# A transformer block on one core: text rows loaded in two parts, patch rows computed directly, and the last 36 keys' three products stacked into one

## The reference

```python
x = jnp.einsum('bnd,ed->bne', x, proj_w) + proj_b + pos_embed     # patches
h = jnp.concatenate([h, txt], axis=1)                             # (8, 164, 192)
xn = layernorm(layernorm(h), ln_w)
Q = xn[:, None] * W_qk[None, :, None, :]                          # 12 heads
attn = softmax(where(causal, Q @ Q.T / sqrt(192), -inf))
out = attn @ (xn - mean(wte, axis=0))                             # wte: 50257 x 192
out = out / arange(1, 165); out = concat_heads(out) @ W_o.T
h = h + out
```

## Time and profile before

| | us |
|---|---|
| median of 3 runs | 373.03 (372.75 to 373.41) |
| the profiled execution | 372.14, its span 370.40 |
| TensorE busy | 332.7 (90% of the span) |
| DVE / ACT / GpSimd busy | 219.9 / 127.9 / 169.0 |
| mean granted TensorE clock | 0.976 |
| bytes moved | 74.29 MB, mean 201 GB/s |

### The profile page before, as it was taken

The page is one execution under the profiler, slowest core; times in us unless marked ns, Lnnn a source line. Parts: engine busy times, 40 slices in busy tenths (PEclk is TensorE's granted clock), DMA queues, the critical chain, the costliest instruction groups (busy, mean ns, idle before and its releaser), DMA issues.

```text
span 370.4 us, 6796 instructions
## 1 busy us (share of the span) xinstructions
PE 332.7 (90%) x2352; PEld 306.4 (83%) x2352; DVE 219.9 (59%) x546; ACT 127.9 (35%) x438; POOL 169.0 (46%) x181
## 2 busy tenths in 40 slices
PE   5886779999799899899899898999949999999992
PEld 1866679989699799799798798999824999999991
DVE  1479638678669679578588888656476222222221
ACT  2065423644643453454436004545720111111110
POOL 3067375583574763862953501450562134444321
PEclk9899889999999999999999999999998999999997
DMA  7399999899799899799797999900223599999930
GB/s 226 114 419 341 215 213 212 236 177 210 221 196 213 225 199 239 191 199 271 162 198 155 295 229 237 230 11 0 84 101 93 165 276 276 273 265 272 273 93 15
DMA packets 20176, 74.29 MB, mean 201 GB/s; under 512 B 3388, under 2 KB 9021, under 8 KB 18874
## 3 DMA queue, kind: packets, MB, share of 16 engines
q0 software_dynamic: 7344, 30.57, 40.8%
q1 hardware_dynamic: 9898, 40.40, 36.8%
q10 hardware_dynamic: 2912, 3.04, 2.9%
HBM read 66.12 MB, written 9.25 MB: 203 GB/s over the span
## 4 chain that ended last, share of the span: by engine, by line
PE 39%; issue 18%; DMA 14%; POOL 14%; DVE 8%; ACT 3%; POOLq 1%; SPq 0%; DVEq 0%; ACTq 0%
PE bO L1198 18%; DMA wbuf<-in_wte 11%; PE bE L1198 10%; PE bS L1198 5%; PE bJ L1198 4%; POOL AwA L390 4%; DMA H<-in_txtA 4%; POOL PA L416 3%; POOL wbuf L401 3%; POOL AwB L390 2%; ACT PA L552 2%; POOL PB L416 1%; DVE negmax L791 1%; PE bT L1544 1%; DVE PTB0L L808 1%
## 5 line engine op out<-in xcount | busy, mean ns | idle before, releaser
L552 ACT ACTIVATE PA<-bS,negmax 128x128 f32<-128x128 f32 x96 | 33.9, 366 | 85.2 <-DVE negmax L791 85.2
L416 POOL TENSOR_TENSOR PA<-PA,rn 128x512 f32<-128x512 f32 x24 | 25.8, 1075 | 64.3 <-DVE rn L803 64.3
L390 POOL TENSOR_TENSOR AwA<-zT,w 96x512 f32<-96x512 f32 x45 | 53.4, 1514 | 3.3 <-ACT zT L534 3.3
L1198 PE MATMUL bJ<-wo_sb,oTA 128*128 128x192 f32 x288 | 51.4, 328 | 0.0
L1198 PEld LDWEIGHTS bS<-zT,AwA 96*128 96x128 f32 x384 | 48.0, 197 | 1.1
L1198 PE MATMUL bS<-zT,AwA 96*128 96x128 f32 x384 | 48.2, 280 | 0.0
L1198 PEld LDWEIGHTS bJ<-wo_sb,oTA 128*128 128x128 f32 x288 | 46.2, 190 | 0.0
L1198 PE MATMUL bO<-PA,wx 96*128 96x112 f32 x384 | 45.4, 275 | 0.5 <-DVE PA L1171 0.5
L1198 PEld LDWEIGHTS bO<-PA,wx 96*128 96x128 f32 x384 | 44.9, 192 | 0.7 <-DVE PA L1171 0.7
L463 POOL DMA_INDIRECT out<-PA,yrow x16 | 15.0, 940 | 56.1 <-DVE PA L1187 56.1
L689 ACT ACTIVATE AwA<-bO 128x448 f32<-128x448 f32 x16 | 8.7, 543 | 78.4 <-PE bO L1198 52.8
(11 more groups left out here) (247 smaller groups left out, 690.9 us busy)
## 6 DMA issues: line engine op xcount, KB each, us to landing
wbuf<-in_wte POOLq DMA_DIRECT2D x20, 1344.0 KB, 13.0
wx<-in_wi SPq DMA_DIRECT2D x16, 576.0 KB
wx<-in_wo SPq DMA_DIRECT2D x16, 576.0 KB
wx<-in_wte SPq DMA_DIRECT2D x6, 1344.0 KB, 8.5
dispatched<-zeros SPq DMA_DIRECT2D x7, 675.5 KB, 10.3
wbuf<-in_wte SPq DMA_DIRECT2D x2, 1344.0 KB, 12.1
AwA<-dispatched ACTq DMA_DIRECT2D x14, 168.9 KB
wo_sb<-in_wo_attn SPq DMA_DIRECT2D x1, 1728.0 KB, 6.9
```

What stands on the lines that cost most here:

```text
L390: nc.gpsimd.tensor_tensor(o, zT[:, k, ss].unsqueeze(1).to_broadcast(list(o.shape)), w2[:, k, hs].unsqueeze(2).to_broadcast(list(o.shape)), ...
L416: nc.gpsimd.tensor_tensor(t, t, q.unsqueeze(2).to_broadcast(list(t.shape)), ALU.mult).then_inc(p_ready, 1)
L552: last = nc.scalar.activation(PA[:, h, :], bank[:, j * SA:(j + 1) * SA], ACT.Exp, bias=negmax[:, h:h + 1], accum_out=lsum[:, h:h + 1])
L1198: return nc.tensor.matmul(o, l, r, start=start, stop=stop, skip_group_check=True)
```

## The change

1. The text rows are loaded as 80 and 12 partitions in place of 92. The patches and their weights are loaded in two halves.
2. TensorE computes the patch rows of batches 0 and 1 directly, without embT. The other batches' transposes stand between score(0, 1) and score(0, 2). Twelve warming products (`stay_warm`) before and behind the first z_transpose are gone. pat_sb, pw_sb and embT lie in expert buffers.
3. The first two table chunks go ahead of wo_attn; SP waits for all of ACT's first constants before them. The matrices for the routing are loaded after the plain chunks, and ACT casts them in batch LAST-1.
4. On GpSimd the weighing stands in front of the table loads. Statistics and factors of batches 2 to 7 move from the start into batch 0.
5. B rows are held three times on 108 partitions (txtB is loaded three times). PB has 108 further columns per group, into which `last_keys` writes the last 36 keys' normalised probabilities three times; p_transpose(b, 4) transposes them at once. In PTB1 and vB the partitions hold high and low parts so that one product with 128 partitions is the sum of all three.

```diff
+SR = 3 * SB
+LV, LP = slice(0, SB), slice(64, 64 + SB)
 def pt_round(q, x, bank):
-            return PTB1[x][0:SB, :, :], bank[0:SB, 0:HEADS * SB]...
+            rows = LP if x else slice(0, SR)
+            return PTB1[rows, :, :], bank[rows, 0:HEADS * SB]...
 # SP
-            sp.dma_start(pw_sb, projw).then_inc(pat_in, 16)
-            sp.dma_start(pat_sb, patches).then_inc(pat_in, 16)
-            sp.dma_start(H[IMG:128, 0:NBATCH, :], txtA).then_inc(txt_in, 16)
+            for part, arrived in ((slice(0, 3), pat_in), (slice(3, 6), pat2_in)):
+                sp.dma_start(pw_sb[:, part, :], projw[:, part, :]).then_inc(arrived, 16)
+                sp.dma_start(pat_sb[:, part, :], patches[:, part, :]).then_inc(arrived, 16)
+            for p0, p1 in ((IMG, 116), (116, 128)):
+                sp.dma_start(H[p0:p1, 0:NBATCH, :], txtA[p0 - IMG:p1 - IMG]).then_inc(txt_in, 16)
+            sp.dma_start(H[0:BP, NBATCH:SLOTS, :], txtBp).then_inc(late_in, 16)
-            sp.wait_ge(hb_in, 16)
+            sp.wait_ge(hb_in, 48)
+            sp.wait_ge(w_in, 32)
-            sp.dma_start(wo_sb[:, :, :], wo_attn).then_inc(wo_in, 16)
             for s in range(WBUF):
                 sp.dma_start(wchunk[s], wv[:, s, :]).then_inc(wte_first, 16)
+            sp.dma_start(wo_sb[:, :, :], wo_attn).then_inc(wo_in, 16)
...
+            plain_loads(sp)
             sp.dma_start(mat32, cst2_d[:, C_MAT:NCST2]).then_inc(mat_in, 16)
-            plain_loads(sp)
 # GpSimd
-                        t, q = PB[:, q0:q0 + 2, :], rn[0:HB * SB, 12 + q0:14 + q0]
+                        t, q = PB[:, q0:q0 + 2, 0:SA], rn[0:HB * SB, 12 + q0:14 + q0]
+            def last_keys():
+                for q0 in (0, 2):
+                    t, k = PB[:, q0:q0 + 2, SEQ:SEQ + SR].rearrange("p q (t s) -> p q t s", t=3), PB[:, q0:q0 + 2, SA:SEQ]
+                    nc.gpsimd.tensor_tensor(t, k.unsqueeze(2).to_broadcast(list(t.shape)),
+                                            rn[0:HB * SB, 12 + q0:14 + q0].unsqueeze(2).unsqueeze(3).to_broadcast(list(t.shape)),
+                                            ALU.mult).then_inc(pb_ready, 1)
-            weigh(0, 1, (1,), range(3))
-            rsqrt(rstd[:, :, 2:NBATCH], nmr[:, :, 2:NBATCH], 2)
-            weigh(0, 1, (1,), (3,))
-            normalise(0, range(1))
+            weigh(0, 1, (1,))
             add_wte(2, 0, 0)
-            normalise(0, range(1, 2))
             add_wte(3, 1, 0)
-            normalise(0, range(2, 3))
+            normalise(0, range(3))
             def iteration(b, i, r):
                 normalise(b, range(3, SPR))
+                weigh(b + 1, n, (0, 1), (0, 1))
+                if r is not None:
+                    add_wte_nth(i, r)
+                last_keys()
+                weigh(b + 1, n, (0, 1), (2,))
+                normalise(b + 1, (0,))
+                if is0(b):
+                    rsqrt(rstd[:, :, 2:NBATCH], nmr[:, :, 2:NBATCH], 2)
+                if r is not None:
+                    add_wte_nth(i, r + 1)
+                normalise(b + 1, (1,))
+                weigh(b + 1, n, (0, 1), (3,))
+                if r is not None:
+                    add_wte_nth(i, r + 2)
+                normalise(b + 1, (2,))
 # ACT
-            act.dma_start(hB[:], txtB).then_inc(hb_in, 16)
+            for t in range(3):
+                act.dma_start(hB[t * SB:(t + 1) * SB, :, :], txtB).then_inc(hb_in, 16)
-                for v, z, n in ((vA, zA, 128), (vB, zB, SB)):
+                for v, z, n in ((vA[0], zA, 128), (vB, zB, SR)):
 # DVE: the first batch
             add_patches(0)
-            dve.wait_ge(txt_in, 16)
+            add_patches(1)
+            dve.wait_ge(txt_in, 32)
             z(0)
-            for j in range(1, 4):
-                add_patches(j)
-            variances(2, NBATCH)
-            row_max(0, 0)
...
+            row_max(0, 0)
             row_max(0, 1)
             row_factor(0, 0)
-            value_low(0)
+            for j in range(2, 5):
+                add_patches(j)
             row_factor(0, 1)
             row_max(0, 2)
+            value_low(0)
             z(1)
             row_factor(0, 2)
-            factors(2, NBATCH, 2)
 # DVE: iteration(b)
                 e_copy(b, 2)
+                if is0(b):
+                    variances(2, NBATCH)
                 plain_sum(b, 0)
                 row_max(b + 1, 0)
...
+                if is0(b):
+                    factors(2, NBATCH, 2)
                 z(b + 2)
 # TensorE
+            def embed_rows(b, k0, k1):
+                for k in range(k0, k1):
+                    last = mm(bT[b][0:IMG, 0:EMB], pat_sb[:, k, b * IMG:(b + 1) * IMG], pw_sb[:, k, :], k == 0, k == 5)
-                            last = nc.tensor.transpose(bank[0:SB, g * HS:(g + 1) * HS], PB[:, g, SA:SEQ], ident[0:HS, 0:HS])
+                            last = nc.tensor.transpose(bank[0:SR, g * HS:(g + 1) * HS], PB[:, g, SEQ:SEQ + SR], ident[0:HS, 0:HS])
-                        mm(oo, vA[x][:, 0:E0], PTB0[y][:, :, :], i == 0, False)
-                        last = mm(oo, vB[x][:, 0:E0], PTB1[y][:, :, :], False, i == 2)
+                        last = mm(oo, vA[x][:, 0:E0], PTB0[y][:, :, :], i == 0, False)
+                if g == 3:
+                    last = mm(oo, vB[:, 0:E0], PTB1[:, :, :], False, True)
-            stay_warm(bS[0], 6)
             z_transpose(0, 0)
-            stay_warm(bS[0], 6)
+            embed(bO[1][0:EC, EF:NBATCH * IMG], 1, EF, NBATCH * IMG).then_inc(emb_ready, 1)
             pe.wait_ge(bf_ready, 3)
-            for r in range(3):
-                score(0, r, r < 2)
+            score(0, 0, True)
+            score(0, 1, True)
+            pe.wait_ge(embT_ready, 2)
+            for j in range(1, 4):
+                token_transpose(j)
+            score(0, 2)
```

## The result

The changed kernel takes 375.96 us (median of 8 runs, 372.65 to 380.05) against 373.22 (372.08 to 373.87), a ratio of 1.0064 with a 95% interval of 1.0040 to 1.0088. The forecast was 356.3 us, with a range of 351 to 364.

A forecast was written before the change was run, and what follows sets the result against it. TensorE's own instructions were taken to bound the loop, plus one GpSimd wait, after a start waiting for data. Savings 4.8 + 2.0 + 2.3 + 6.2 + 1.4 = 16.7 from 372.14 gave 355.4, plus 0.89 for the median: 356.3 us, range 351 to 364.

The forecast's parts named there:

- Settled batches, 4 x 1.56: Four settled batches: each 1.56 us shorter (0.84 + 0.92 - 0.2), so -6.2 us in all.
- the 12 us pair: GpSimd's table loads reusing a slot after 12 us: only these could land late, by some 2 us; charged 0.
- Removal of the AwA wait and the 0.84 us of products: TensorE per batch: the 0.92 us wait for AwA goes, and value(b,3) saves 0.84 us of products.
- The start, -4.8: Up to the first PB normalisation: 35.4 us in place of 40.23, -4.8 us (bounds -0.5 and -6.5).
- Rival B: The start gains little: txtB's copies land at 12.5 us, zA at 20.0; 360.5 us in all; chance 0.10.
- Batch 0, 27.6: First interval of PB normalisations: 27.6 us in place of 29.63, without the chunk stall but with variances added; -2.0 us.
- Batch 1, 24.6: Second interval: 24.6 us in place of 26.89, the mat cast moving to where ACT waits anyway; -2.3 us.
- Behind the loop, -1.4: After the settled batches: two more shortened value(b,3), worth 0.84 and 0.6, so -1.4 us.
- A: The loop: the accumulating stream becomes the bound, 25.6 us a batch, five intervals lose 1.0; 361 us; chance 0.12.
- C: value(b,3): products saved do not shorten the loop, since it waits on other steps; seven times 0.84, 362 us; chance 0.07.
- D: TensorE's clock near z_transpose(0): idle time lowers it, two scores cost 2.8 us more; 359.1 us; chance 0.08.
- E: Slower: a batch's first load finds its slot not landed, TensorE stops at p_transpose(b,4), 4.8 us each; chance 0.07.

The follow-up runs named there:

- e2: The changed kernel with a second buffer for the plain table chunks; 363.78 us, ratio 0.975.
- e1: The changed kernel with GpSimd's three table loads back in front of the weighing and normalisations, one plain buffer; 370.76 us, ratio 0.997.
- e9: The kernel before with two buffers for the plain chunks and nothing else; 374.37 us, ratio 1.005.
- e10: The changed kernel, one plain buffer, with row_max(b+1,0) in front of plain_sum(b,0) on DVE; 367.48 us, ratio 0.984.
- e3: The kernel before with part 5 of the change alone (the stacked last keys); 373.19 us, ratio 1.002.
- e7: e2 with part 5 undone: one copy of txtB, three products again, no last_keys; 365.71 us, ratio 0.982.
- e12: e5 with last_keys in front of GpSimd's first table load of a batch; 357.77 us, ratio 0.958.
- e4: e2 with txtB's three loads behind the constants and statistics of only two batches before the patches; 364.27 us, ratio 0.977.
- e6: e4 with last_keys in front of GpSimd's first table load of a batch; 367.19 us, ratio 0.983.
- e14: e12 with only the variances' last instruction, nmr, moved behind row_max(1,1); 359.89 us, ratio 0.962.
- e8: e5 with the variances of batches 2 to 7 moved behind row_max(1,1); 361.65 us, ratio 0.970.
- e13: e12 with the variances of batches 2 to 7 moved behind row_max(1,1); 359.91 us, ratio 0.966.
- a0: The changed kernel, unedited, measured and profiled again; 380.13 us, ratio 1.014.
- e5: e2 with the three copies of txtB laid out in the input and loaded by one transfer; 362.81 us, ratio 0.973.

## Why the prediction was wrong

- **Settled batches, 4 x 1.56: failed, and the largest error** (7.2 us, with 3.3 in batch 1). The step is "What is late next? ... Only the 12 us pair can be late ... I take 0". It looked at GpSimd's own slots and not at the other load of the table. The sum was at hand: before, 16.5 us from the first plain_sum of a batch to the next issue (101.30 to 117.78) and 8.4 of landing are 24.9 of 26.2. Of the 16.5, the changed kernel needs 14.7, which with 8.4 would be 23.1; at the forecast's 24.6 only 1.5 are left, and the loads were moved towards the plain one, which then took 11.5. Shown by e2, e1, e9 and e10. The cycle accounts for the settled batches at full clock (26.06 on average); the rest of the 26.41 is the clock behind the wait that the cycle makes.
- **Removal of the AwA wait and the 0.84 us of products: right.** No wait for AwA in the changed kernel; 0.85 us in e3, 0.92 per batch between e7 and e2. With the cycle opened, settled batches take 24.39 (forecast 24.6).
- **The start, -4.8: failed,** got -1.1. Rival B was right: the copies landed at 12.23, near the upper bound of 12.5, and not at 9.7. The mis-sized term is "1.2 us more at 378 GB/s": the engines were full, but at 190 to 209 GB/s from 8 to 12 us. With it fell "should come by 11 too": ln landed at 16.2, and DVE's patch addition (16.85, forecast 13.4) stood behind it. zA(0) is 3.7 us later than forecast, and that is the whole of what the first normalisation lacks. That the path from zA(0) to it came out as forecast (18.25 us, forecast 18.2) is luck: at full clock it takes 16.7, and the changed kernel's clock filled the difference. Without the copies (e7) the first normalisation is at 35.73 us, with the forecast at 35.4, at a reduced clock too.
- **Batch 0, 27.6: mis-sized by 3.9.** The 2.2 us of variances are there (2.31 in e12). The forecast took nmr's 0.76 us as a price of its own, where it is 0.17 or 2.8 by what GpSimd does; and it left out that the clock falls behind a wait of 2.3 us (0.60 over 4 us in e12). Of the 3.1 us between the changed kernel and e12, nmr is 2.6. I put the 0.8 between 27.6 and e12's 28.41 down to the clock; this is argued, not shown.
- **Batch 1, 24.6:** right once the cycle is open (24.28 to 24.54 in e2, e4 to e6, e12, e14; 25.6 to 26.0 in e8 and e13, behind nwz).
- **Behind the loop, -1.4:** not reached. The rest is 168.5 to 175.8 us over all kernels. In the long ones the experts' weights land later (11.6 us in the changed kernel, 6.7 in e7, by the list of transfers from 245 us on), and TensorE waits for them: 2.3 us in the changed kernel, 1.1 in e2, nothing in e7 and e12. Another 2.0 us are 39 matmuls into bJ in the routing, which take 12.3 us in the changed kernel, 10.3 before and 8.9 in e12; the clock over these 20 us is 0.83, 0.91 and 1.00. The two about make up the 4.0 by which the rest is longer than before. The kernels built on the one before had 168.9 to 170.9. Whether the change makes the long rest more frequent stays open; no experiment was made on it.
- **Rivals.** A fell (e2: 230 GB/s at 24.4 us). C was half right: beside GpSimd's old order only 0.33 of 0.84 us arrive (e3), in good surroundings all (e7). D, to which I gave under 0.5 us on the path, came true at its own place in the changed kernel's profile (1.5 us between zA(0) and score(0,0), though not in a0's), and besides in batch 0 and in some later batches, as a follower of long waits. E named the right kind of event, a transfer not landed, with the wrong transfer: of the 7% for slower none stood for what happened. Its own mechanism shows in e5's batch 0, 1.97 us of TensorE at the fourth transposes.

With three edits more (a second plain buffer, one load for the copies, last_keys in front of the load) the terms of the forecast nearly all hold: e12 has its first normalisation at 35.74, then 28.41, 24.28, 24.45 and a rest of 168.5, and takes 357.77 us, 0.958 of before. It beats both kernels. The buffer's part in this is shown, the one load's by zA(0), the third edit's is not.

## What to carry to other kernels

When a change shortens a loop, list every closed cycle in it, the buffers' too (landing, use, release, next issue), with its length now, and compare each with the forecast length and not with the present one; moving transfers in time changes the landing of all others in flight. Where small vector instructions stand on the critical path beside GpSimd's work, give them a price with and without it. A part that saves time on the bounding engine is worth its price only after the wait right behind it has been looked at: test it alone and in the final surroundings, the two can differ by a factor of three.

## What the runs showed that I had not expected

- The same 1344 KB plain load lands in 7.6 or 11.5 us (e1, changed), the accumulating ones in 11.4 and 11.0.
- A transfers' share of 1.00 to 1.09 goes with 190, 230 or 378 GB/s (10 to 12 us of the changed kernel, a settled stretch of e2): the share alone doesn't tell whether the limit is reached.
- Three loads of 36 rows each let work start at 12.23 us (12.2 to 13.4 in five profiles), one of 112 rows, of the same size within 4%, at 10.34 (9.4 to 10.3 in five).
- DVE instructions of 12 elements per partition: 0.17 us, or 2.79 (nmr) and 3.81 (nwz) beside GpSimd; one of four (rn in e8): 2.20.
- The same kernel at the same place ran at full or at reduced clock (changed and a0 before score(0,0)), for 1.5 us; an interval from one profile can be off by that.
